# Local attention: the band mask is added by VectorE in PSUM, in place of four TensorE products per tile

## The chip, the cores and the metric

The kernel runs on one core of a Trainium2 chip. The metric is the device time of one execution in microseconds (us); the median of the runs shown counts. A core has TensorE (PE, matrix products, which only write to PSUM), VectorE (DVE), ScalarE (ACT), GpSimd (POOL) and the queue of SyncE (SP) that issues DMA. The engines run on their own instruction streams, each in its order, and meet at semaphores.

## The reference, cut to what matters

The whole is a stack of gated cross-attention layers on x (4, 512, 256) and, as the feed-forward of the last of them, a local transformer of 6 layers. The change concerns its attention: 16 heads of 64 numbers, windows of 64 tokens, each window looking at itself and at the one before it.

```python
def local_attention(q, k, v):
    ...
    bk2, bv2 = (look(bk), look(bv))     # the window before, and the window itself
    ...
    mask = (it < jb) | (it > jb + w) | (jb == -1)
    sim = jnp.einsum('bhwie,bhwje->bhwij', bq, bk2) * QK_SCALE
    sim = jnp.where(mask, -jnp.finfo(sim.dtype).max, sim)
    attn = jax.nn.softmax(sim, -1)
    out = jnp.einsum('bhwij,bhwje->bhwie', attn, bv2)
    return out.reshape(b, h, n, d)
```

A query may see the keys from 64 tokens back up to itself. Around it stand, per layer: `qkv = x @ Wqkv`, l2-norm and rotary embedding of q and k, the output product with `Wo`, and a feed-forward part with layer norm and a gelu gate.

## The kernel before

The kernel has two parts that follow each other. `first_part` does the cross-attention layers and the other feed-forwards; no line of it is touched. `last_part` does the local transformer, from about 2315 us to the end. The change lies in it alone.

**Tiles.** A unit `(d, g, b)` is a layer, a group of four heads and a batch; it has four tiles `tt` of 128 tokens (two windows). That makes 6 x 4 x 4 x 4 = 384 tiles. The order runs through half a layer at a time (two batches, four groups, four tiles each: 32 tiles), so the pattern of work repeats 12 times. I call one such stretch a round.

**Stages of a tile**, each a name in `last_order`, with how many turns after its start it comes: `qkv` (lag 0), `rot` (1), `tr` (3), `sc` and `ex` (4), `pt` (5), `pv` (6), `ot` (7). One turn of the program handles one tile of each stage, so TensorE's stream in a turn is: `wo` (output product, once per unit), `sc`, `tr`, `ot`, `pv`, `pt`, what the feed-forward has in that turn (`fh`, `fw`, the norm), and last `qkv`, which is 12 products (L1300).

**The scores.** `sc` on TensorE first writes the mask and then adds the products to it:

```python
for w in range(2):
    for e in range(2):
        half = slice(64 * e, 64 * e + 64)
        tensor.matmul(psum[64 * w:64 * w + 64, b0 + e, 0:2 * P], ident_b[half, half],
                      bc(band[half, 1 if tt else 0, w, :], 1, 2), start=True, stop=False)
```

These are four products of 64x64 by 256 columns in bf16 (L1318; `w` is the window, `e` the head's parity), one for each quadrant of the array. Eight products of queries by keys follow in fp32 (L1323; 16 instructions in the trace). DVE then takes the maximum per head (L1453, written to a spare corner of PSUM), waits for itself (`step.join()`), and multiplies it into the bias of the exponential (L1457). ACT does four exponentials (`ex`, L1573). The scores have one slot of two banks (`two`), so `sc` of the next tile waits on TensorE for `ex` of this one.

**DVE's stream in a turn**: `wo` (two additions into the residual, L1478), `sc` (L1453, L1457), `rot` (sum of squares, L1447), `ot` (L1471), `pv` (L1464, L1466), the feed-forward's pieces (`fg`: L1510 and the cast L1515), `qkv` (three rotary products, L1439 to L1441), and `lq` (casts of new weights, L1423). **ACT's stream**: `tr` (L1561, L1566), `ot` (L1585), `ex` (L1573), `pt` (L1578), gelu (L1610), `qkv` (copies of v at L1546 to L1551 and the squares L1554, which wait for L1441 and free the bank of q and k). After a gelu the exponential needs its table again: ACT_TABLE_LOAD. **POOL** adds the two rotary parts (L1629), takes the power for the norm (L1633), scales k (L1636) and makes low parts (L1652, L1625).

Six further PSUM banks (`one`) go round in fixed order among `qkv`, `tr`, `pt`, `pv`, `ot`, `wo` and the feed-forward; a stage waits for the engine that last emptied its bank.

Of the kernel before, what the change touches and what calls it, by code (L numbers as in the profile page):

```python
# [7 lines left out]
ALU = mybir.AluOpType  # L8
# [4 lines left out]
BF16 = mybir.dt.bfloat16  # L13
# [4 lines left out]
P = 128  # L18
# [38 lines left out]
def bc(ap, axis, n):  # L57

    dims = [list(d) for d in ap.ap]
    return bass.AP(ap.tensor, ap.offset, dims[:axis] + [[0, n]] + dims[axis:])  # L60
# [1008 lines left out]
def weights_of(d, g, b):  # L1069

    return d, 1 if b >= B // 2 and g < 2 else 0, g
# [54 lines left out]
def last_part(nc, a, at, s):  # L1126

    tensor, vector, scalar, gpsimd, sync = nc.tensor, nc.vector, nc.scalar, nc.gpsimd, nc.sync
    PE, V, A, G, SP = at.PE, at.V, at.A, at.G, at.SP
    vec, sm, psum, tokens = at.vec, at.sm, at.psum, at.tokens  # L1130
    ident, ident_b, ones_mean = at.ident, at.ident_b, at.ones_mean
    order = last_order()
    S_ = {name: s(name) for name in (
        "xs_act xs_pool lq_dve lq_pool rt_dve qk_pe qkv_pe sq_act qkv_act qkv_dve rot_dve rot_pool tr_pe tr_act sc_pe sc_dve ex_act "
        "pt_pe pt_act pv_pe pv_dve ot_pe ot_act ot_dve add_pe add_dve fo_pool fa_pe fa_dve fa_act fa_pool fb_pe fb_dve fb_pool fy_pe fy_dve fc_act fc_dve "
        "fgate_pe fh_pe fh_act fg_dve fi_dve fg_pool fw_pe fx_dve band_in rt_in zeroed fin_dve kept_in written").split()}
    staged_in = [s(f"staged_in{i}") for i in range(2)]
    step = at.step

    with ExitStack() as p2:  # L1140
        def psb(name, shape, dt=F32):
            return p2.enter_context(nc.sbuf_tensor(name, shape, dt))
# [5 lines left out]
        staged = psb("staged", [P, 2, STAGED])  # L1148
        scales = psb("scales", [P, 2, LHD])
        rotary = psb("rotary", [P, 2, 2, QT, 2, LHD])  # L1150
        band = psb("band_bias", [P, 2, 2, P], BF16)
        keys = psb("keys", [P, 1, C, 9 * WIN])
        vals, mixed = psb("vals", [P, 6, 4, LHD + 1]), psb("mixed_vals", [P, 7, 4, LHD + 1])
        queries = psb("queries", [P, 1, C, P])
# [63 lines left out]
        def left(got, key, waits):  # L1218

            before = got[key][1]  # L1220
            if before:
                waits.wait_ge(S_[before[0]], before[1])
# [7 lines left out]
        def stat(name, u):  # L1230
            return stats[:, stat_at[name, u][0], :]
# [5 lines left out]
        def chunk(u):  # L1237

            kind, j = u[0], u[-1]
            if kind == "f":  # L1240
                to = [w[:, j * STAGED:(j + 1) * STAGED] for w in (w12_hi, w12_lo)]
                return a["w12"][u[1]][:, j * STAGED:(j + 1) * STAGED], to
            src = a["quads"][u[1], u[3]]
            if kind == "q":
                to = [w[:, wqkv_at[u[1:4]][0], j * STAGED:(j + 1) * STAGED] for w in (wqkv_hi, wqkv_lo)]
                return src[:, j * STAGED:(j + 1) * STAGED], to
            return src[:, QW:QW + 2 * D], [w[:, wout_at[u[1:4]][0], :] for w in (wout_hi, wout_lo)]
# [12 lines left out]
        def tok(tt):  # L1260
            return slice(tt * P, (tt + 1) * P)
# [11 lines left out]
        def soft(u):  # L1273
            return small_stats[:, soft_at["soft", u][0], :]

        def window_keys(n, e, pair, w):

            even, odd = (w // 2, 4 + w // 2) if w % 2 == 0 else (w // 2, 5 + w // 2)
            part = keys[64 * e:64 * e + 64, n, pair, even * WIN:(even + 1) * WIN]
            dims = [list(d) for d in part.ap]  # L1280
            return bass.AP(part.tensor, part.offset, [dims[0], [(odd - even) * WIN, 2], [1, WIN]])
# [2 lines left out]
            return ap[lo:hi, :, 0:LHD]  # L1284

        def tensor_program():
            PE.wait_ge(S_["band_in"], 16)
            PE.wait_ge(S_["zeroed"], 1)
            for stage, u in order.walk():
                if stage == "qkv":  # L1290
                    d, g, b, tt = u
                    w = weights_of(d, g, b)
# [3 lines left out]
                    for i, (to, lo, hi, sem) in enumerate(((qk, 0, 512, "qk_pe"), (vp[:, 0:256], 512, COLS, "qkv_pe"))):  # L1296
                        left(one, ("qkv", u, i), PE)
                        for c in range(C):
                            for n, (x_, w_) in enumerate(((xs_hi, wh), (xs_hi, wl), (xs_lo, wh))):
                                ins = tensor.matmul(to, x_[:, c, b % 2, tok(tt)], w_[:, c * COLS + lo:c * COLS + hi],  # L1300
                                                    start=c == 0 and n == 0, stop=c == C - 1 and n == 2)
# [8 lines left out]
                elif stage == "sc":  # L1310
                    tt = u[3]
                    PE.wait_ge(S_["tr_act"], at_("tr", u))
                    left(two, u, PE)
                    b0, n, q = two[u][0], key_at["kT", u[:3]][0], queries[:, qry_at["q", u][0], :, :]
                    for w in range(2):
                        for e in range(2):
                            half = slice(64 * e, 64 * e + 64)
                            tensor.matmul(psum[64 * w:64 * w + 64, b0 + e, 0:2 * P], ident_b[half, half],  # L1318
                                          bc(band[half, 1 if tt else 0, w, :], 1, 2), start=True, stop=False)
                    for pair in range(2):  # L1320
                        for w in range(2):
                            for e in range(2):
                                ins = tensor.matmul(psum[64 * w:64 * w + 64, b0 + e, tok(pair)],  # L1323
                                                    q[64 * e:64 * e + 64, pair, 64 * w:64 * w + 64],
                                                    window_keys(n, e, pair, 2 * tt + w), start=False, stop=pair == 1)
                    ins.then_inc(S_["sc_pe"], 1)
                elif stage == "pt":
                    PE.wait_ge(S_["ex_act"], at_("ex", u))
# [22 lines left out]
                elif stage == "wo":  # L1351
                    d, g, b = u
                    PE.wait_ge(S_["ot_dve"], at_("ot", u + (QT - 1,)))
                    w = weights_of(d, g, b)
# [49 lines left out]
        def vector_program():  # L1404
# [4 lines left out]
            for stage, u in order.walk():  # L1409
# [22 lines left out]
                elif stage == "qkv":  # L1432
                    d, g, b, tt = u
# [14 lines left out]
                elif stage == "sc":  # L1448
                    st, y = soft(u), stat("norm", u)[:, 8:12]
                    V.wait_ge(S_["sc_pe"], at_("sc", u))  # L1450
                    left(soft_at, ("soft", u), V)
                    top = psum[:, two[u][0], 2 * P:2 * P + 4].rearrange("p (e j) -> p e j", e=2)
                    step(vector.tensor_reduce(top, scores(u), AX.X, ALU.max))  # L1453
# [14 lines left out]
                elif stage == "ot":  # L1468
                    d, g, b, tt = u
# [183 lines left out]
                                         ALU.subtract).then_inc(S_["fg_pool"], 1)  # L1653

        def sync_program():
            sync.dma_start(band[:, :, :, :], a["band"]).then_inc(S_["band_in"], 16)
            for stage, u in order.walk():
                if stage == "lq":
                    slot = stage_at["lq", u][0]
                    left(stage_at, ("lq", u), SP)  # L1660
                    sync.dma_start(staged[:, slot, :], chunk(u)[0]).then_inc(staged_in[slot], 16)
                elif stage == "rt":
                    if u:
                        SP.wait_ge(S_["rt_dve"], u)
                    if u > 1:
                        SP.wait_ge(S_["qkv_dve"], at_("qkv", (u - 2, 0, B - 1, QT - 1)))
                    sync.dma_start(rotary[:, u % 2], a["rotary"]).then_inc(S_["rt_in"], 16)
                    sync.dma_start(scales[:, :, :], a["qk_scale"][u]).then_inc(S_["rt_in"], 16)
                elif stage == "kb":
                    if u:  # L1670
                        SP.wait_ge(S_["written"], 16 * C * at_("fin", u - 1))
                    for c in range(C):
                        sync.dma_start(back[:, c, :], at.x_kept[c * P:(c + 1) * P, u, :]).then_inc(S_["kept_in"], 16)
                elif stage == "fin":
                    for c in range(C):
                        SP.wait_ge(S_["fin_dve"], C * (at_("fin", u) - 1) + c + 1)
                        sync.dma_start(at.out[c * P:(c + 1) * P, u, :], back[:, c, :]).then_inc(S_["written"], 16)
            SP.wait_ge(S_["written"], 16 * C * B)

        tensor_program()  # L1680
        vector_program()
        scalar_program()
        gpsimd_program()
        sync_program()


# [4 lines left out]
def build(nc, a, out):  # L1691
    ctx = ExitStack()
    with ctx:
# [67 lines left out]
        for w in (PE, V, A, G, SP):  # L1761
            w.wait_ge(at.over, B)
        last_part(nc, a, at, s)


# [6 lines left out]
def lay_out(i):  # L1772
# [5 lines left out]
    a = {}  # L1778
# [42 lines left out]
    bf16 = i["L1_ffn_kernel"].dtype  # L1821
# [3 lines left out]
    n, h = S, LHD // 2  # L1825
    half = np.arange(0, LHD, 2, dtype=np.float32)
# [11 lines left out]
    own, prev = np.where(j_ <= i_, 0.0, MASKED), np.where(j_ >= i_, 0.0, MASKED)  # L1838
    rows = [np.concatenate([own, np.full((WIN, WIN), MASKED)], 1), np.concatenate([own, prev], 1)]
    tiles = np.stack([np.stack([r, np.concatenate([prev, own], 1)]) for r in rows])  # L1840
    a["band"] = np.ascontiguousarray(np.tile(tiles.transpose(2, 0, 1, 3), (2, 1, 1, 1))).astype(bf16)
    qs = np.stack([i["L3_ffn_q_scale"], i["L3_ffn_k_scale"]], 1)
    a["qk_scale"] = np.ascontiguousarray(np.broadcast_to(qs[:, None], (DEPTH, P, 2, LHD)))
    wqkv = i["L3_ffn_Wqkv"].reshape(DEPTH, D, 3, 4, 4 * LHD).transpose(0, 3, 1, 2, 4).reshape(DEPTH, 4, D, 12 * LHD)
# [4 lines left out]
    for k in range(2):  # L1849
        w = np.zeros((DEPTH, D, HT * P), np.float32)  # L1850
# [19 lines left out]
```

## Time and profile before

| | |
|---|---|
| median of three runs | 5177.25 us (5173.41 to 5180.86) |
| span of the profiled execution | 5182.7 us |
| busy over the span: PE, DVE, ACT, POOL | 93%, 66%, 60%, 46% |
| tiles of local attention | 384, from about 2333 us to the end |

The profiled execution is 5.4 us longer than the median of the runs. In the profile "busy" of PE counts from the start of each product to a modelled end, so that it contains short gaps. An idle time has behind it, after `<-`, what ended it; "issue" is time in which nothing shown was waited for.

### The profile page before, as it was taken

How to read it: one execution, taken by the hardware profiler on the slowest of the kernel's cores; microseconds unless marked ns; L12 is line 12 of the kernel's file. 1: busy time of each engine (PE TensorE's matmuls, PEld its weight loads, DVE VectorE, ACT ScalarE, POOL GpSimd, SP SyncE). 2: the span in 40 equal slices, each digit the busy share in tenths (PEclk: the TensorE clock that was granted, in tenths of full speed). 3: DMA queues.
4: the chain of work that ended last, by engine and by line, in shares of the span. 5: the costliest groups of instructions: out<-in, count | busy, mean ns of one | idle time of the engine just before them, and what ended most of it. 6: DMA issues, size and time to landing. Idle time of an engine off the chain costs nothing.

```text
span 5182.7 us, 92467 instructions
## 1 busy us (share of the span) xinstructions
PE 4823.6 (93%) x35414; PEld 3013.7 (58%) x35480; DVE 3429.4 (66%) x6514; ACT 3112.6 (60%) x6618; POOL 2409.7 (46%) x2314
## 2 busy tenths in 40 slices
PE   6898999989899898969999999999999999999998
PEld 2232333334334343227877777777777777777776
DVE  4766566676675857757766666666666666666664
ACT  3565555434344444547777677776777677777763
POOL 3211101111011111129777677676767677776762
PEclk8999999999999899989999999999999999999998
DMA  5233222322312222311000000000000000000000
GB/s 121 52 56 59 54 44 55 65 50 48 61 37 50 46 57 43 56 30 46 8 18 26 16 24 20 22 22 20 22 18 24 18 28 16 24 19 19 24 22 21
DMA packets 125161, 188.97 MB, mean 36 GB/s; under 512 B 18896, under 2 KB 67664, under 8 KB 124496
## 3 DMA queue, kind: packets, MB, share of 16 engines
q1 hardware_dynamic: 124720, 183.06, 15.9%
q8 instruction: 281, 4.60, 0.4%
q14 instruction: 160, 1.31, 0.1%
HBM read 150.09 MB, written 32.51 MB: 35 GB/s over the span
## 4 chain that ended last, share of the span: by engine, by line
PE 64%; DVE 14%; ACT 8%; POOL 7%; issue 6%; DMA 1%; SPq 0%; DVEq 0%; POOLq 0%; ACTq 0%
PE psum L1253 16%; PE psum L1300 10%; PE psum L467 4%; PE psum L432 4%; PE psum L453 4%; DVE maxes L655 3%; PE psum L1308 3%; PE psum L1341 3%; PE psum L1332 2%; PE psum L414 2%; PE psum L1323 2%; POOL stats L1633 2%; PE psum L476 2%; ACT probs L836 2%; PE psum L422 1%
## 5 line engine op out<-in xcount | busy, mean ns | idle before, releaser
L836 ACT ACTIVATE probs<-psum 128x1024 f32<-128x1024 f32 x768 | 772.2, 1019 | 609.9 <-PE psum L453 337.7
L655 DVE TENSOR_REDUCE maxes<-psum 128x1 f32<-128x1024 f32 x512 | 616.5, 1212 | 246.6 <-PE psum L432 242.5
L1633 POOL TENSOR_TENSOR stats<-stats,minus_half 128x8 f32<-128x8 f32 x384 | 651.8, 1697 | 32.0
L1439 DVE TENSOR_TENSOR lwork<-psum,rotary 128x512 f32<-128x512 f32 x384 | 264.2, 688 | 513.1 <-PE psum L1300 446.9
L1573 ACT ACTIVATE lprobs<-psum,small_stats,stats 128x128 f32<-128x128 f32 x1536 | 581.1, 474 | 12.3 <-DVE small_stats L1457 11.5
L1629 POOL TENSOR_TENSOR lwork<-lwork 128x512 f32<-128x512 f32 x384 | 493.9, 1286 | 202.9 <-DVE lwork L1441 202.7
L1300 PE MATMUL psum<-wqkv_hi,xs_hi 128*128 128x512 f32 (+1 forms) x1536 | 554.6, 361 | 33.6 <-POOL xs_lo L1620 17.1
L453 PE MATMUL psum<-stack 98*128 98x512 bf16 x1536 | 513.1, 390 | 72.1 <-DVE maxes L655 32.0
L432 PE MATMUL psum<-stack 96*128 96x512 bf16 x1536 | 473.2, 391 | 64.2 <-ACT probs L836 53.1
L1300 PE MATMUL psum<-wqkv_hi,xs_lo 128*128 128x512 f32 (+1 forms) x1536 | 519.6, 338 | 0.0
L1300 PE MATMUL psum<-wqkv_lo,xs_hi 128*128 128x512 f32 (+1 forms) x1536 | 519.3, 338 | 0.0
L957 POOL TENSOR_TENSOR attn<-attn,sums 128x512 f32<-128x512 f32 x48 | 60.9, 1268 | 948.4 <-DVE sums L688 948.4
L467 PE MATMUL psum<-probs,values 128*32 128x512 f32 x3072 | 428.2, 631 | 0.7 <-ACT probs L836 0.6
L1546 ACT ACTIVATE vals<-psum 128x256 f32<-128x256 f32 x384 | 152.9, 398 | 452.6 <-PE psum L1300 451.2
L652 DVE CUSTOM_DVE_ANT_0 psum<-psum,mask_by_query 128x1024 f32<-128x1024 f32 x256 | 314.1, 1228 | 151.9 <-PE psum L432 150.2
L453 PEld LDWEIGHTS psum<-stack 98*128 98x128 bf16 x1536 | 135.9, 100 | 427.9 <-issue 183.2
L1300 PEld LDWEIGHTS psum<-wqkv_hi,xs_hi 128*128 128x128 f32 x1536 | 291.1, 190 | 96.9 <-issue 33.5
L432 PEld LDWEIGHTS psum<-stack 96*128 96x128 bf16 x1536 | 131.6, 99 | 357.9 <-ACT probs L836 131.3
L1300 PEld LDWEIGHTS psum<-wqkv_lo,xs_hi 128*128 128x128 f32 x1536 | 291.5, 190 | 42.1 <-issue 5.3
L1300 PEld LDWEIGHTS psum<-wqkv_hi,xs_lo 128*128 128x128 f32 x1536 | 290.3, 189 | 33.4
L1554 ACT ACTIVATE lwork<-psum 128x512 f32<-128x512 f32 x384 | 225.6, 587 | 135.7 <-DVE lwork L1441 133.5
L1447 DVE TENSOR_REDUCE stats<-lwork 128x8 f32<-128x512 f32 x384 | 263.4, 686 | 26.8 <-ACT lwork L1554 23.0
(225 smaller groups left out, 11526.7 us busy)
## 6 DMA issues: line engine op xcount, KB each, us to landing
stack<-k_parts SPq DMA_DIRECT2D x288, 128.0 KB
staged<-in_quads SPq DMA_DIRECT2D x144, 256.0 KB, 3.0
k_parts<-parts SPq DMA_DIRECT2D x48, 384.0 KB, 2.9
stack<-q_parts SPq DMA_DIRECT2D x288, 64.0 KB
staged<-in_w SPq DMA_DIRECT2D x54, 256.0 KB, 2.7
ctx<-in_ctxT SPq DMA_DIRECT2D x24, 512.0 KB, 4.7
q_parts<-parts SPq DMA_DIRECT2D x24, 384.0 KB, 2.3
arena<-in_ctxT SPq DMA_DIRECT2D x8, 512.0 KB, 4.8
```

The lines of the kernel that those rows point to most:

```text
L432: ins = tensor.matmul(ps[:, i, :], q[0:STACK, h, qt * P:(qt + 1) * P], k[0:STACK, h, i * S:(i + 1) * S], start=True, stop=True)
L453: ins = tensor.matmul(ps[:, i, :], ky[0:STACK + 2, h, kt * P:(kt + 1) * P], q[0:STACK + 2, h, :], start=True, stop=L != 1)
L467: ins = tensor.matmul(bank(acc)[32 * h:32 * h + 32, :], values[:, kt, 4 * g + h, :], pr, start=kt == 0, stop=kt == KT - 1)
L652: ins = vector.tensor_tensor_reduce(out=scores, in0=scores, in1=masks_q[:, qt * S2:(qt + 1) * S2], scale=1.0, scalar=-3e38, op0=ALU.add, o ...
L655: ins = vector.tensor_reduce(to, pair(("M", u)), AX.XY, ALU.max)
L836: scalar.activation(probs[:, i % 6, :, :], pair(("E", u)), ACT.Exp).then_inc(S_["E_act"], 1)
L1253: ins = tensor.matmul(ps, l, r, start=first and n == 0, stop=last and n == 2)
L1300: ins = tensor.matmul(to, x_[:, c, b % 2, tok(tt)], w_[:, c * COLS + lo:c * COLS + hi], start=c == 0 and n == 0, stop=c == C - 1 and n == 2)
L1439: vector.tensor_tensor(v4(t1), v4(qk), bc(rotary[:, d % 2, 0, tt], 2, 4), ALU.mult)
L1573: ins = scalar.activation(pr[:, h, :], scores(u)[:, h % 2, h // 2, :], ACT.Exp, bias=st[:, 4 + h:5 + h], scale=y[:, h:h + 1])
L1629: gpsimd.tensor_tensor(t1, t1, t2, ALU.add)
L1633: pool_step(gpsimd.tensor_tensor(st[:, 8:16], st[:, 0:8], minus_half[:, :], ALU.pow))
```

## The change

The four products that write the mask are gone; the eight products of queries by keys now each start afresh (`start=True, stop=True`). `band` is laid out by rows of the tile, 128 partitions by 128 columns for each of its two forms, and holds the same values (0 and -1e30, bf16). On DVE `sc` gets one more instruction, which adds `band`, spread over the four heads, to the 512 columns of scores in place in PSUM, and a join, so that the maximum waits for it. The wait for the DMA of `band` moves from TensorE to DVE. No other stage is moved.

```diff
-            PE.wait_ge(S_["band_in"], 16)
             PE.wait_ge(S_["zeroed"], 1)
...
-                    for w in range(2):
-                        for e in range(2):
-                            half = slice(64 * e, 64 * e + 64)
-                            tensor.matmul(psum[64 * w:64 * w + 64, b0 + e, 0:2 * P], ident_b[half, half],
-                                          bc(band[half, 1 if tt else 0, w, :], 1, 2), start=True, stop=False)
                     for pair in range(2):
                         for w in range(2):
                             for e in range(2):
                                 ins = tensor.matmul(psum[64 * w:64 * w + 64, b0 + e, tok(pair)],
                                                     q[64 * e:64 * e + 64, pair, 64 * w:64 * w + 64],
-                                                    window_keys(n, e, pair, 2 * tt + w), start=False, stop=pair == 1)
+                                                    window_keys(n, e, pair, 2 * tt + w), start=True, stop=True)
                     ins.then_inc(S_["sc_pe"], 1)
...
                     st, y = soft(u), stat("norm", u)[:, 8:12]
                     V.wait_ge(S_["sc_pe"], at_("sc", u))
+                    V.wait_ge(S_["band_in"], 16)
+                    of_tile = bc(bc(band[:, 1 if u[3] else 0, :], 1, 2), 1, 2)
+                    step(vector.tensor_tensor(scores(u), scores(u), of_tile, ALU.add))
+                    step.join()
                     left(soft_at, ("soft", u), V)
                     top = psum[:, two[u][0], 2 * P:2 * P + 4].rearrange("p (e j) -> p e j", e=2)
                     step(vector.tensor_reduce(top, scores(u), AX.X, ALU.max))
...
-            sync.dma_start(band[:, :, :, :], a["band"]).then_inc(S_["band_in"], 16)
+            sync.dma_start(band[:, :, :], a["band"]).then_inc(S_["band_in"], 16)
```

DVE's rows around the scores of one tile, in the kernel before:

```order
L1478 TENSOR_TENSOR x_resid<-psum,x_resid 128x512 [waits add_pe]
L1478 TENSOR_TENSOR x_resid<-psum,x_resid 128x512
L1453 TENSOR_REDUCE psum<-psum 128x4 [waits pv_dve,sc_pe]
L1457 SCALAR_TENSOR_TENSOR small_stats<-psum,stats 128x2x2 [waits vector_step]
L1447 TENSOR_REDUCE stats<-lwork 128x8 [waits ex_act,sq_act]
```

The same place in the changed kernel, where lines have other numbers:

```order
L1476 TENSOR_TENSOR x_resid<-psum,x_resid 128x512 [waits add_pe]
L1476 TENSOR_TENSOR x_resid<-psum,x_resid 128x512
L1447 TENSOR_TENSOR psum<-psum,band_bias 128x2x256 [waits sc_pe]
L1451 TENSOR_REDUCE psum<-psum 128x4 [waits pv_dve,vector_step]
L1455 SCALAR_TENSOR_TENSOR small_stats<-psum,stats 128x2x2 [waits vector_step]
L1441 TENSOR_REDUCE stats<-lwork 128x8 [waits ex_act,sq_act]
```

The wait for the scores has gone from the maximum to the addition, and the maximum waits for DVE's own step. On ACT nothing is added; its rows at the exponential, in a turn that follows a gelu, are in the kernel before:

```order
L1585 ACTIVATE att_hi<-psum 128x2x128 [waits ot_pe]
L1573 ACT_TABLE_LOAD
L1573 ACTIVATE lprobs<-psum,small_stats,stats 128x128 [waits sc_dve]
L1573 ACTIVATE lprobs<-psum,small_stats,stats 128x128 x3
L1578 ACTIVATE turned<-psum 128x512 [waits pt_pe]
```

The load of the table stands ahead of the wait for DVE.

## Rows read from the trace of the kernel before

**Rows 1.** The page: span, and busy time of each engine.

```profile
span 5182.7 us, 92467 instructions
PE 4823.6 (93%) x35414; PEld 3013.7 (58%) x35480; DVE 3429.4 (66%) x6514; ACT 3112.6 (60%) x6618; POOL 2409.7 (46%) x2314
```

**Rows 2.** Busy time by stretch, local attention: us, busy us (instructions), PEclk, DMA share, GB/s.

```profile
2700.00:5100.00 2400.00, 2350.43 (x22207) 1883.79 (x22206) 1613.65 (x3690) 1704.72 (x4497) 1711.56 (x1676) 1.00 0.07 21
```

**Rows 3.** Waits in 2700 to 5100 us: who waited for whom, us in total, times, longest.

```profile
DVE lwork L1439 <- PE psum L1300: 393.9, 145, 6.1
PE psum L1318 <- ACT lprobs L1573: 18.6, 51, 0.4
ACT lprobs L1573 <- DVE small_stats L1457: 8.9, 17, 2.0
```

**Rows 4.** PE in order of time, one tile's scores: start us, us, engine, line, operation.

```profile
3535.51 0.30 PE L1318 MATMUL psum<-band_bias,ident_b 64*64 64x256 bf16 x4
3535.63 0.62 PE L1323 MATMUL psum<-keys,queries 64*64 64x128 f32 x16
```

**Rows 5.** Groups by line in 2700 to 5100 us: busy us, mean ns of one, idle before.

```profile
L1318 PE MATMUL psum<-band_bias,ident_b 64*64 64x256 bf16 x1300 | 98.5, 293 | 18.6 <-ACT lprobs L1573 18.6
L1478 DVE TENSOR_TENSOR x_resid<-psum,x_resid 128x512 f32<-128x512 f32 x164 | 105.5, 686 | 103.3 <-PE psum L1253 103.3
```

**Rows 6.** In order of time, DVE, ACT and PE, a tile far from feed-forward work.

```profile
3210.34 0.16 DVE L1457 SCALAR_TENSOR_TENSOR small_stats<-psum,stats 128x4 f32<-128x4 f32 x1
3212.48 0.69 DVE L1439 TENSOR_TENSOR lwork<-psum,rotary 128x512 f32<-128x512 f32 x1 [0.50 <-PE psum L1300]
...
3210.53 1.51 ACT L1573 ACTIVATE lprobs<-psum,small_stats,stats 128x128 f32<-128x128 f32 x4
...
3213.08 0.30 PE L1318 MATMUL psum<-band_bias,ident_b 64*64 64x256 bf16 x4
```

**Rows 7.** DVE in order of time, two tiles after a gelu.

```profile
3055.75 0.69 DVE L1453 TENSOR_REDUCE psum<-psum 128x4 f32<-128x512 f32 x1
3056.47 0.16 DVE L1457 SCALAR_TENSOR_TENSOR small_stats<-psum,stats 128x4 f32<-128x4 f32 x1
...
3060.27 0.68 DVE L1439 TENSOR_TENSOR lwork<-psum,rotary 128x512 f32<-128x512 f32 x1
3060.87 0.41 DVE L1440 TENSOR_TENSOR lwork<-psum,rotary 128x256 f32<-128x256 f32 x1
...
3061.53 0.69 DVE L1453 TENSOR_REDUCE psum<-psum 128x4 f32<-128x512 f32 x1
3062.26 0.16 DVE L1457 SCALAR_TENSOR_TENSOR small_stats<-psum,stats 128x4 f32<-128x4 f32 x1
```

**Rows 8.** ACT and PE in order of time, the same two tiles.

```profile
3056.82 1.28 ACT L1573 ACT_TABLE_LOAD   x1
3058.11 1.50 ACT L1573 ACTIVATE lprobs<-psum,small_stats,stats 128x128 f32<-128x128 f32 x4
...
3062.98 1.54 ACT L1573 ACTIVATE lprobs<-psum,small_stats,stats 128x128 f32<-128x128 f32 x4
...
3059.67 0.30 PE L1318 MATMUL psum<-band_bias,ident_b 64*64 64x256 bf16 x4 [0.38 <-ACT lprobs L1573]
...
3064.66 0.30 PE L1318 MATMUL psum<-band_bias,ident_b 64*64 64x256 bf16 x4
```

**Rows 9.** Two other places of the round: DVE at 3033; ACT and PE at 3162.

```profile
3033.01 0.69 DVE L1447 TENSOR_REDUCE stats<-lwork 128x8 f32<-128x512 f32 x1 [0.27 <-issue]
...
3162.72 1.54 ACT L1573 ACTIVATE lprobs<-psum,small_stats,stats 128x128 f32<-128x128 f32 x4
...
3164.49 0.30 PE L1318 MATMUL psum<-band_bias,ident_b 64*64 64x256 bf16 x4
```

**Rows 10.** In order of time, a wait of PE for a bank, and what leads to it.

```profile
3132.75 0.42 DVE L1471 TENSOR_TENSOR att_lo<-psum,att_hi 128x256 fp32r<-128x256 f32 x1 [0.18 <-ACT att_hi L1585]
...
3138.39 0.60 ACT L1554 ACTIVATE lwork<-psum 128x512 f32<-128x512 f32 x1 [1.32 <-DVE lwork L1441]
...
3139.04 0.50 PE L1300 MATMUL psum<-wqkv_hi,xs_hi 128*128 128x512 f32 x1 [0.71 <-ACT lwork L1554]
```

More of the change, by code:

```diff
@@ L1150, in last_part @@
         rotary = psb("rotary", [P, 2, 2, QT, 2, LHD])
-        band = psb("band_bias", [P, 2, 2, P], BF16)
+        band = psb("band_bias", [P, 2, P], BF16)
         keys = psb("keys", [P, 1, C, 9 * WIN])
@@ L1840, in lay_out @@
     tiles = np.stack([np.stack([r, np.concatenate([prev, own], 1)]) for r in rows])
-    a["band"] = np.ascontiguousarray(np.tile(tiles.transpose(2, 0, 1, 3), (2, 1, 1, 1))).astype(bf16)
+    a["band"] = np.ascontiguousarray(tiles.transpose(1, 2, 0, 3).reshape(P, 2, P)).astype(bf16)
     qs = np.stack([i["L3_ffn_q_scale"], i["L3_ffn_k_scale"]], 1)
```

## The prediction

> **What bounds the kernel now.** I read the page first, then the local attention's stretch alone, then the waits in it, then single tiles in order of time. The page has PE at 93% and DVE at 66% of a span of 5182.7 us [rows 1]. In the stretch that the change touches PE is busy for 2350 of 2400 us at a granted clock of 1.00 (the 2.4 GHz level), DVE for 1614, ACT for 1705 and POOL for 1712 [rows 2]. So TensorE sets the pace there, and whatever leaves its stream is worth its full time wherever PE is not waiting for anyone. The waits show the other half: DVE waits for PE's qkv products in 145 turns of some 325, for 394 us [rows 3]. In the other turns it is behind PE, with work queued. And PE already waits for an exponential 51 times, 18.6 us in all, which is about five times in each round of 32 tiles [rows 3]. The reader is to look, place by place, at how far the chain scores, maximum, exponential, next scores is from PE's own pace. The change shortens PE's part and lengthens DVE's part of that chain.
>
> **What is removed: four products.** Their rows say 293 ns each [rows 5], but the four run at once in their quadrants and the next products do not wait for their ends: the first product of queries by keys starts 0.12 us after the first of the four, 3535.63 against 3535.51 [rows 4]. That is what a tile gives back, 0.12 us; 384 tiles would make 46 us if PE waited nowhere. As bounds I take 0.10, the same with a slightly longer first load of fp32 weights now in the open, and 0.30, the length of the group's whole row [rows 4]. I take 0.12, since the distance of two starts leaves out the modelled ends.
>
> **What is added: one DVE instruction and its join.** Before has no in-place addition in PSUM. The nearest row is the residual's addition, a 128x512 fp32 operation with one PSUM operand, 686 ns [rows 5]. With a join behind it the next instruction starts 0.73 us after (the maximum at 3061.53, its successor at 3062.26), where without one two rotary products start 0.60 apart (3060.27 and 3060.87) [rows 7]. The maximum must wait for the sum, so I take 0.73 per tile. The bounds are 0.60, as if the join were free, and 1.0, an estimate: one operation's 0.69 plus half again for reading and writing the same bank, which no row shows. Over 384 tiles that is 280 us more of DVE, on 3429 [rows 1]; it makes DVE 74% over the stretch (1614 + 325 x 0.73 = 1851 of 2400), so that DVE doesn't become the bound as a whole. The question is where it is late already.
>
> The Trainium skill (VectorE: DVE Perf Modes, "The DRAIN you can't avoid") says that the next DVE instruction starts only when the pipe is empty, and that a semaphore between two costs nothing extra. The two distances above, 0.60 and 0.73, disagree with it in this case. By that rule with the unjoined distance, the addition would cost 0.60, and the sum below would come out 12 us lower, at 5172; I keep the row with the join.
>
> **Where the addition is covered.** Behind the addition wait the maximum, L1457, everything else of DVE's turn, ACT's exponential, and through it PE's next scores; through DVE's rotary products (L1439 to L1441) ACT's squares, and through them a bank for PE; and POOL's sums. In a tile far from feed-forward work [rows 6] the exponential ends at 3212.04 and PE comes for the slot at 3213.08: 1.04 us of cover for 0.73. DVE then waits 0.50 for PE before L1439, so that about 0.2 us, and the 0.12 by which PE is earlier, are carried on; the next such wait or the next long turn takes them. In turns with feed-forward products or the output product DVE waits for microseconds (394 us in 145 waits, rows 3), and all is absorbed. If this cover were gone, each tile would cost 0.6. In the turn right after a gelu, PE waits for the exponential (0.38 at 3059.67), but there the load of the table, 1.28 us, stands ahead of the wait for DVE [rows 8]: L1457 ends at 3056.63, the exponential starts at 3058.11, and 1.48 us of cover are enough.
>
> **Where it is not covered.** The second tile after a gelu. DVE runs from the maximum at 3055.75 to the one at 3061.53 without a wait [rows 7], since it has two pieces of the gate between. Two additions fall into this stretch, 1.46 us. Their cover is what lies between L1457's end (3062.42) and the exponential (3062.98), 0.56, less 0.04 for the handover, and between the exponential's end (3064.52) and PE's scores (3064.66), 0.14, less 0.05 [rows 8]. That leaves 1.46 - 0.52 - 0.09 = 0.85 us late for PE, and PE is the pace here, so that it is not made up. A round has four such places. At 3001 to 3012 the rows repeat these two covers: 0.85. At 3162 the second cover is 0.23 instead of 0.14 [rows 9]: 0.76. At 3033 there are 0.27 us of idle DVE in between [rows 9]: 0.58. The sum is 3.0 us per round, 36 us over 12 rounds.
>
> Besides, PE waits 0.71 for a bank that ACT's squares free, and these wait 1.32 for DVE's L1441 [rows 10]. One addition lies ahead of it and 0.18 of a DVE wait covers it (and some 0.05 more): 0.5 late, 6 us over 12 rounds.
>
> **The sum.** The 0.12 is realised in the 24 tiles of a round that are not part of one of the four chains: 24 x 0.12 x 12 = 35 us less. So 36 + 6 - 35 = 7 us more. Of the profiled 5182.7 that makes 5189.7, and since that execution stood 5.4 us above the median of the runs, 5184.
>
> The moved wait for the mask's DMA costs nothing: it was issued at the head of the last part, and the first scores come four turns later. POOL gets the sums of squares up to 0.73 later and has one more turn until PE needs its result. What first_part does is unchanged.
>
> **Rivals.**
> (a) *The mask's products occupy PE longer than the two starts say.* If a tile gives back 0.24 (between 0.12 and the row's 0.30 [rows 4]), the gain is 24 x 0.24 x 12 = 69 and the price the same 42: 27 us less, 5150. For it: 0.12 is about the streaming of 256 columns alone, and a change of operand type at the switch may cost something. Against it: the distance is the same wherever I looked at a tile.
> (b) *The covers hold.* The four places lose nothing because the delay moves phases of POOL and DVE or because DVE takes the slack elsewhere: 384 x 0.12 = 46 less, 5131. For it: PE's long turns reset DVE. Against it: in rows 7 DVE has no gap at all. A milder form of it is the free join, 12 us less than the forecast.
> (c) *The addition costs more than 0.73, and DVE is behind in every short turn.* Decisive price: in the short turn of rows 6 DVE has 0.50 us of its own plus what PE leaves; from 0.9 us on each short turn hands on its delay instead of absorbing it. At 1.0 us the four places cost 4 x (2.0 - 0.61) less 0.36 = 5.2 per round and the bank place 0.8, 72 us in 12 rounds, against 35: 37 us more, 5214. For it: reading and writing the same PSUM bank has no row. Against it: the residual's addition shows no surcharge for its PSUM operand.
> (d) *More places are uncovered than four.* DVE was behind PE in over half of the turns (180 of 325, rows 3). If two more tiles of a round lose 0.6 each, it is 14 us more than the forecast, 5198.
>
> **How the numbers follow.** About 0.2% (10 us) is what a measurement of this kernel can tell from no change. The forecast, with its neighbours from the free join to one place more (5172 to 5192), has a chance of 0.45; (d) 0.20; (c) 0.13; (a) 0.14; (b) 0.08. The forecast's own spread reaches past 5187 with a third of its chance. Faster by over 0.2% (below 5167): (a) and (b), 0.22. Slower by over 0.2% (above 5187.6): (c), (d) and some 0.07 of the forecast's, 0.40. The rest is 0.38. The range from 5145 to 5216 holds (a), the forecast, (d) and the price in (c), and leaves out (b) and the far end of (c).
>
> **What would show it.** Scores of a tile starting about 0.12 earlier behind the last qkv product confirms the gain; the distance from the addition's start to the maximum's should be 0.73. PE's wait for the exponential should grow from 18.6 us to some 50 in the same stretch, at four new places per round, and the wait of L1300 for the squares by 0.5 at one. DVE's wait for L1300 should shrink by over 150 us. I am wrong if PE waits for the exponential in quiet tiles as well, or if the addition takes over 0.8.

## The result, and the profile after

| | before | changed |
|---|---|---|
| median of the runs | 5178.91 us | 5224.27 us |
| span of the profiled execution | 5182.7 us | 5224.8 us |

The changed kernel is slower, by under 1% but clear of noise. The ratio is 1.0085, 95% interval 1.0071 to 1.0099: 44 us more, 37 to 51. That lies outside the range from 5145 to 5216.

The page after, and the stretch of local attention alone (us, busy us of PE, PEld, DVE, ACT, POOL, granted clock, DMA share, GB/s), which answer to [rows 1] and [rows 2]:

```profile
span 5224.8 us, 89780 instructions
PE 4812.3 (92%) x33878; PEld 2985.4 (57%) x33944; DVE 3652.1 (70%) x6898; ACT 3134.0 (60%) x6618; POOL 2409.9 (46%) x2314
...
2700.00:5100.00 2400.00, 2310.08 (x20588) 1835.47 (x20587) 1774.31 (x3959) 1703.89 (x4445) 1699.53 (x1665) 1.00 0.07 21
```

PE is busy 40 us less in 2400, at the same granted clock of 1.00 (the 2.4 GHz level), so the clock has no part in it. The first scores start within 4 us of where they did; the whole loss comes after. The waits of the same stretch, which answer to [rows 3]:

```profile
DVE lwork L1433 <- PE psum L1299: 332.9, 101, 5.3
ACT lprobs L1571 <- DVE small_stats L1455: 76.1, 119, 2.7
PE psum L1299 <- ACT lwork L1552: 28.9, 51, 0.9
PE psum L1317 <- ACT lprobs L1571: 20.0, 80, 0.4
PE psum L1253 <- ACT lwork L1552: 14.2, 29, 0.9
```

PE's wait for the exponential has hardly grown, from 18.6 to 20.0 us, though it comes 80 times instead of 51. What has grown is PE's wait for the squares (lwork, L1552), which free a bank. In the kernel before these were:

```profile
PE psum L1300 <- ACT lwork L1554: 15.6, 27, 0.7
PE psum L1341 <- ACT lwork L1554: 5.2, 20, 0.3
PE psum L1253 <- ACT lwork L1554: 1.1, 5, 0.2
```

To see where the time went I compared the distance from one tile's first score product to the next one's in both traces, tile by tile, and took the mean over ten rounds (the second to the eleventh, 320 distances). Tiles of a round are counted from 0.

| place in the round | 4 | 5 | 6 | 9 | 12 | 20 | 22 | 25 | 28 | 18 places, each | all 32 |
|---|---|---|---|---|---|---|---|---|---|---|---|
| change, us per round | +0.62 | +0.72 | +0.25 | +0.88 | +0.98 | +0.57 | -0.34 | +0.38 | +0.82 | -0.07 or -0.08 | +3.9 |

Seven places (4, 5, 9, 12, 20, 25, 28) lose 5.0 us per round, and place 6 another 0.25. The five places that the table leaves out (1, 3, 14, 21, 26) add 0.3 together. A tile in which PE waits for nobody is 0.07 shorter, not 0.12. Twelve rounds of 3.9 make 47 us; the first round loses nothing, and from the first scores to the end the changed kernel takes 46 us more.

Three of these means hide two kinds of round. A round is half a layer, and the two halves differ. In second halves place 25 loses 1.16 and place 22 loses 0.22; in first halves they gain 0.40 and 0.91. Place 9 loses 0.60 in second halves and 1.16 in first ones. The reason at places 22 and 25 is told below, under "Two places where a cast is in play".

**The gain.** PE in order of time, a tile away from feed-forward work, first before, then after (start us, us):

```profile
3213.08 0.30 PE L1318 MATMUL psum<-band_bias,ident_b 64*64 64x256 bf16 x4
3213.21 0.61 PE L1323 MATMUL psum<-keys,queries 64*64 64x128 f32 x16
3213.75 0.33 PE L1308 MATMUL psum<-ident,lwork 128*128 128x128 f32 x1
```

```profile
3209.61 0.67 PE L1317 MATMUL psum<-keys,queries 64*64 64x128 f32 x16
3210.20 0.33 PE L1307 MATMUL psum<-ident,lwork 128*128 128x128 f32 x1
```

From the first product to the transposes behind it takes 0.67 before and 0.59 after. The products by the keys themselves took 0.54 before and take 0.59 now: the 0.13 of the mask's products covered 0.05 or 0.06 of them. The first loads of fp32 weights used to run beside the mask's products and now stand in the open; in the starts of single products the first group of four holds the array for 0.16 us, each later one for 0.11.

**The addition** costs what was forecast. DVE after, two tiles behind a gelu:

```profile
3061.55 0.69 DVE L1447 TENSOR_TENSOR psum<-psum,band_bias 128x512 f32<-128x512 f32 x1
3062.27 0.70 DVE L1451 TENSOR_REDUCE psum<-psum 128x4 f32<-128x512 f32 x1
```

0.72 us from start to start, and no surcharge for reading and writing one bank.

**The loss, at place 12** (the second tile after a gelu, [rows 7, 8] before). ACT and PE before, then after:

```profile
3061.65 0.60 ACT L1554 ACTIVATE lwork<-psum 128x512 f32<-128x512 f32 x1 [1.03 <-DVE lwork L1441]
...
3061.76 0.66 PE L1332 MATMUL psum<-ident,lprobs 128*128 128x128 f32 x4
3062.39 0.47 PE L1300 MATMUL psum<-wqkv_hi,xs_hi 128*128 128x512 f32 x1
```

```profile
3068.19 0.60 ACT L1552 ACTIVATE lwork<-psum 128x512 f32<-128x512 f32 x1 [1.84 <-DVE lwork L1435]
...
3068.93 0.47 PE L1299 MATMUL psum<-wqkv_hi,xs_hi 128*128 128x512 f32 x1 [0.86 <-ACT lwork L1552]
```

After, the squares end at 3068.79 and PE starts its qkv products 0.14 later. Before, they end at 3062.25, and PE starts 0.14 later as well, at 3062.39. So PE was waiting for this bank already, and no row said so: the transposes in front of it (L1332) have a modelled end at 3062.42, later than the next start, so that no idle time shows. Their starts show it. In the quiet tile of [rows 6] qkv follows the transposes at 0.42 (3210.39 and 3210.81), here at 0.63. The cover was nil. (A cover is the time by which something may come late before anyone waits for it.) At place 28 the same holds of the products of the feed-forward; before, then after:

```profile
3183.84 0.60 ACT L1554 ACTIVATE lwork<-psum 128x512 f32<-128x512 f32 x1 [1.02 <-DVE lwork L1441]
...
3183.97 0.66 PE L1332 MATMUL psum<-ident,lprobs 128*128 128x128 f32 x4
3184.49 0.50 PE L1253 MATMUL psum<-hid_hi,w_hi 128*128 128x512 f32 x1
```

```profile
3192.81 0.60 ACT L1552 ACTIVATE lwork<-psum 128x512 f32<-128x512 f32 x1 [1.82 <-DVE lwork L1435]
...
3193.46 0.50 PE L1253 MATMUL psum<-hid_hi,w_hi 128*128 128x512 f32 x1 [0.75 <-ACT lwork L1552]
```

0.05 from the squares' end to PE in both (3184.44 and 3184.49; 3193.41 and 3193.46), and the forecast had this turn among the long ones that absorb everything.

The same reading at all seven places: in the changed kernel PE starts 0.05 us (5, 9, 25, 28) or 0.14 us (4, 12, 20) after the end of the squares, in round after round, so PE is held by their bank at each of them. In the kernel before the distance is already 0.14 at place 12 and 0.05 at place 28. At place 20 it is 0.39, which leaves 0.25 of cover. At place 4 it is 0.5 in half of the rounds and 0.14 in the others, and place 9 has 0.18 of cover in half of them and none in the rest. What makes the handover 0.05 at one place and 0.14 at another the runs do not show.

**Two places where a cast is in play.** Before, a DVE cast of the gate's result (L1515) took 1.55 us instead of 0.43 in 17 of its executions: at place 22 in every round but the first, just ahead of place 25 in first halves of a layer, and once more in the last round. Each time a GpSimd row of L1652 starts within 4 ns of it; in 11 others that row starts some 40 ns later, and the cast takes 0.43. The cast makes DVE's rotary products late and so the squares' bank. Before, place 25:

```profile
2923.41 1.55 DVE L1515 CAST hid_hi<-lwork 128x512 fp32r<-128x512 f32 x1
2923.41 1.27 POOL L1652 TENSOR_TENSOR hid_lo<-lwork,hid_hi 128x512 fp32r<-128x512 f32 x1
...
2926.91 0.50 PE L1300 MATMUL psum<-wqkv_hi,xs_hi 128*128 128x512 f32 x1 [0.69 <-ACT lwork L1554]
```

In the changed kernel the two no longer start together, and all 17 are gone. In second halves others come up: ahead of place 25 the cast takes 0.70, and at place 22 a cast of weights takes 1.47, with a GpSimd row that started 0.04 to 0.09 ahead of it, and PE waits for another result of DVE. After, place 22:

```profile
3144.23 1.48 DVE L1417 CAST wqkv_hi<-staged 128x512 fp32r<-128x512 f32 x1
...
3148.24 0.50 PE L1253 MATMUL psum<-att_hi,wout_hi 128*128 128x512 f32 x1 [0.88 <-DVE att_lo L1469]
```

So the 44 us contain a gain that comes from shifted starts and not from the mask.

### The profile page after: what moved, and what is told of

It is laid out like the page before. It is cut to its first block, busy times and chain, and to the rows that moved or that the text cites. A ratio compares the mean times of both kernels' runs of the same rounds, so it can differ in the third digit from the quotient of the medians.

```text
span 5224.8 us, 89780 instructions
## 1 busy us (share of the span) xinstructions
PE 4812.3 (92%) x33878; PEld 2985.4 (57%) x33944; DVE 3652.1 (70%) x6898; ACT 3134.0 (60%) x6618; POOL 2409.9 (46%) x2314
## 4 chain that ended last, share of the span: by engine, by line
PE 57%; DVE 22%; issue 7%; ACT 7%; POOL 6%; DMA 1%; SPq 0%; DVEq 0%; POOLq 0%; ACTq 0%
PE psum L1253 16%; PE psum L1299 8%; PE psum L467 4%; PE psum L432 4%; PE psum L453 4%; DVE maxes L655 3%; PE psum L414 2%; DVE psum L1451 2%; POOL stats L1631 2%; PE psum L476 2%; PE psum L1335 2%; DVE psum L1447 2%; PE psum L1326 2%; DVE lwork L1433 2%; ACT probs L836 2%
## 5 line engine op out<-in xcount | busy, mean ns | idle before, releaser
L1552 ACT ACTIVATE lwork<-psum 128x512 f32<-128x512 f32 x384 | 225.7, 588 | 183.1 <-DVE lwork L1435 181.4
L1317 PE MATMUL psum<-keys,queries 64*64 64x128 f32 x6144 | 256.4, 282 | 29.5 <-ACT lprobs L1571 23.3
```

## The experiments

The theory from the traces: PE pays where it waits without cover for a bank that ACT's squares free, since the addition delays DVE's rotary products; the removal brings 0.07 per tile. The rivals: the price is paid through the exponential, as forecast; or the addition harms all tiles (a busier DVE, PSUM contended).

### Removal alone, addition alone

The changed kernel without its addition (the mask is left out), and the kernel before with the addition too.

```diff
                     V.wait_ge(S_["sc_pe"], at_("sc", u))
-                    V.wait_ge(S_["band_in"], 16)
-                    of_tile = bc(bc(band[:, 1 if u[3] else 0, :], 1, 2), 1, 2)
-                    step(vector.tensor_tensor(scores(u), scores(u), of_tile, ALU.add))
-                    step.join()
                     left(soft_at, ("soft", u), V)
```

> The changed kernel without its addition and join: the band mask is left out altogether, so this is the removal of the four products alone. In the trace of the changed kernel a covered tile's turn is 0.07 us shorter than before, not 0.12. If that is all a tile gives back, the time is 384 x 0.07 = 27 us below before, near 5152. If the forecast's 0.12 held, 46 us below, near 5133. If leaving out the products itself did harm, it would be at or above before.

Measured: 0.9963 (0.9950 to 0.9976), 19 us less, 12 to 26. In its trace 19 of the 32 places of a round are 0.07 shorter. The others give 0.05 at most or lose (place 6 0.17, places 12 and 28 0.08), which makes 1.05 us per round, 13 us in twelve. Its profiled execution is 19 us shorter than the one before, and 6 of these stand ahead of the first scores, in code that is the same. The 27 us lie at the upper end, and the forecast's 46 are out.

> The kernel before with the addition and its join on VectorE as in the change, the four products kept (the mask is added twice, which leaves the result as it is). If gain and price add up (gain 27 of removal alone, 45 net), the price alone is about 72: near 5250. If the shorter TensorE turn itself makes VectorE late and so causes part of the price, the addition alone costs less, 45 to 60: 5225 to 5240. The forecast's own price of 42 would give 5221.

Measured: 1.0097 (1.0082 to 1.0112), 50 us more. The same places pay (4: 0.54, 5: 0.71, 9: 0.81, 12: 0.90, 20: 0.49, 25: 0.35, 28: 0.74 per round), places 3 and 6 lose 0.15 and 0.24, place 22 gains 0.26, and the rest keep their length to 0.05 us, most of them to 0.01. A price in all tiles is thereby excluded. By the runs the two parts add to 31 against 44 of the change, with some 7 of uncertainty on each of the three. The traces leave less of a gap: -1.05 and +4.70 us per round add to 3.65 against 3.90, 3 us in twelve rounds. So the two parts nearly add; five of the seven places pay 0.07 or 0.08 more when PE comes earlier.

### Ahead of the exponential or behind it

First with an operation of two inputs in SBUF (`back` is a buffer that only the last layer uses):

```diff
+                    if u[0] < DEPTH - 1:
+                        V.wait_ge(S_["band_in"], 16)
+                        spare = back[:, 0, :].rearrange("p (h n) -> p h n", h=4)
+                        step(vector.tensor_tensor(spare, spare, bc(band[:, 1, 0, :], 1, 4), ALU.max))
+                        step.join()
```

> The kernel before with one addition-like operation of the same size (128x512 fp32, in SBUF, joined) ahead of the maximum, in the 320 tiles of the first five layers. Both theories: 5/6 of what the addition alone costs, some 60 us, 5239, if reading and writing PSUM in place has no price of its own. If it has, this comes out clearly lower than 5/6 of the addition alone.

> The same operation, but behind the last instruction of the scores on VectorE, so that the exponential of the tile doesn't wait for it, while the rotary products, ScalarE's squares and the bank they free do. If the price is paid through VectorE's whole turn and the bank (the theory from the trace of the changed kernel), it costs nearly what it costs ahead of the maximum, 45 to 60 us. If it is paid on the way scores, maximum, exponential, next scores, as forecast, it costs under half of that, below 30 us.

Measured: 1.0164 (1.0147 to 1.0181), 85 us more ahead; 1.0169 (1.0154 to 1.0184), 88 us behind. That is far above what was expected (some 60 ahead; 45 to 60, or below 30, behind), and twice the 42 that are 5/6 of the addition's 50. So the probe itself was not clean. Its rows, ahead and behind (duration in ns: minimum, median, maximum):

```profile
L1455 DVE TENSOR_TENSOR x_back<-x_back,band_bias x320: 671/685/1826, 2332.7 to 4703.6; 128x512 f32<-128x512 f32 x160
```

```profile
L1463 DVE TENSOR_TENSOR x_back<-x_back,band_bias x320: 681/1173/3473, 2331.1 to 4709.0; 128x512 f32<-128x512 f32 x160
```

An operation of 0.69 us took up to 3.5. The pair was repeated with a maximum over 512 columns of SBUF, which has one input:

```diff
+                    if u[0] < DEPTH - 1:
+                        step(vector.tensor_reduce(back[:, 1, 0:8], back[:, 0, :].rearrange("p (h n) -> p h n", h=8), AX.X, ALU.max))
+                        step.join()
```

> The kernel before with one more maximum over 512 columns of SBUF (one input only, joined, the same 0.69 us) ahead of the maximum of the scores, in the 320 tiles of the first five layers. The operation with two inputs in SBUF cost 84 us at this place, and its own rows grew to 0.86 us on average where GpSimd was at work. If that contention was the surplus, this one costs 5/6 of the addition in PSUM alone, 42 us: 5220. If working in place in PSUM saves or costs something, it lies off that.

> The same operation behind the last instruction of the scores. The exponential of the tile no longer waits for it, the rotary products and ScalarE's squares do. If TensorE pays for the bank that the squares free, this costs 30 to 42 us, nearly what it costs ahead. If it pays for the exponential, below 15 us.

Measured: ahead 1.0093 (1.0077 to 1.0108), 48 us more; behind 1.0083 (1.0069 to 1.0096), 43 us more. Here every instance took 668 to 687 ns. Ahead of the maximum it costs 5/6 of the addition (42 us) within the noise, so that working in place in PSUM shows no price of its own. Behind it costs nearly the same, where the path through the exponential would have given below 15. The waits of both in 2700 to 5100 us, ahead first, then behind:

```profile
ACT lprobs L1577 <- DVE small_stats L1461: 58.4, 101, 2.3
PE psum L1300 <- ACT lwork L1558: 22.7, 40, 1.1
PE psum L1318 <- ACT lprobs L1577: 21.4, 74, 0.4
```

```profile
PE psum L1300 <- ACT lwork L1558: 22.8, 40, 1.2
PE psum L1318 <- ACT lprobs L1577: 17.7, 50, 0.4
ACT lprobs L1577 <- DVE small_stats L1458: 10.2, 20, 2.0
```

Behind, the exponential is as free as in the kernel before (10.2 us of waits, against 8.9 in [rows 3]), and PE waits for the squares' bank as long as ahead. The path through the exponential is thus worth about the 5 us between the two, with some 10 of uncertainty; at place 12, where it should matter most, the operation costs 0.88 ahead and 0.71 behind in the first five layers. The bank is the price.

### A narrow addition

The kernel before with an addition over 64 columns.

```diff
+                    narrow = scores(u)[:, :, 0, 0:32]
+                    step(vector.tensor_tensor(narrow, narrow, bc(band_rows[:, 1 if u[3] else 0, 0:32], 1, 2), ALU.add))
+                    step.join()
```

> The kernel before with a joined addition over 64 columns in place of 512 ahead of the maximum (the mask twice in those columns, which changes nothing): some 0.2 us of VectorE per tile. By the covers of the forecast (0.6 us behind the two tiles after a gelu) it costs nothing: within 3 us of before. If at seven places of a round TensorE waits for a bank without any cover, it costs 7 x 0.2 x 12 = 17 us.

Measured: 1.0017 (1.0008 to 1.0026), 9 us more, between the two expectations. It took 0.26 us with its join. Place by place it settles what the total doesn't: places 12 and 28 lose 0.27 and 0.28 per round, the full price, so these have no cover at all. Place 20 loses 0.03, as its cover of 0.25 says. Places 4, 5 and 9 lose 0.10 to 0.12 on the mean: 4 and 5 lose 0.2 in second halves of a layer and nothing in first ones, 9 loses 0.05 and 0.18. Place 6 loses 0.19. Place 25 gains 0.42, for in first halves its cast takes 0.43 here instead of 1.55 and brings 1.02. The bank at place 12, ACT and PE:

```profile
3053.33 0.60 ACT L1559 ACTIVATE lwork<-psum 128x512 f32<-128x512 f32 x1 [1.30 <-DVE lwork L1442]
...
3054.07 0.47 PE L1301 MATMUL psum<-wqkv_hi,xs_hi 128*128 128x512 f32 x1 [0.25 <-ACT lwork L1559]
```

The same 0.14 from the squares' end to PE as in both kernels.

### Half the addition, and twice

The half adds the mask to two of the four heads and leaves the others unmasked; for twice, the addition and its join stand there a second time, which leaves the result as it is. The edit of the half:

```diff
-                    of_tile = bc(bc(band[:, 1 if u[3] else 0, :], 1, 2), 1, 2)
-                    step(vector.tensor_tensor(scores(u), scores(u), of_tile, ALU.add))
+                    half_of = psum[:, two[u][0]:two[u][0] + 2, 0:P]
+                    step(vector.tensor_tensor(half_of, half_of, bc(band[:, 1 if u[3] else 0, :], 1, 2), ALU.add))
```

> The changed kernel with the mask added to two of the four heads only (256 columns, some 0.47 us with its join); the other two heads go unmasked. Without an addition the time was 19 us below before, with the whole one 45 above. If the price is VectorE's time at places without cover, it is linear in between: 19 below plus 0.47 x 88 us per us, 22 above, near 5201. If a part of the price is the additional join and instruction itself, it lies higher, above 5210.

> The changed kernel with the joined addition twice (the mask twice, which leaves the result as it is). If only the same places pay, 0.73 us more at seven places of a round is 61 us more: 5285. If covers of up to 1 us at other places are used up by now, the slope is steeper: 5300 to 5340. Below 5260 would speak against a price paid in VectorE's time.

Measured: half 1.0021 (1.0011 to 1.0030), 11 us more than before; twice 1.0370 (1.0356 to 1.0385), 192 us more. Against DVE's additional time per tile:

| added on DVE per tile, us | 0 | 0.46 | 0.73 | 1.46 |
|---|---|---|---|---|
| against before, us | -19 | +11 | +44 | +192 |
| slope to the next, us per us | 65 | 122 | 203 | |
| in the traces, us per round | -1.05 | +1.10 | +3.90 | +16.25 |

Against what was expected of the half, the price is not linear: it lies below the 22 of the straight line, and it bends upward as covers run out. At 1.46 the covered places pay too (place 0: 0.39, place 18: 1.06, place 31: 0.56 per round), and the steeper of the two expectations was still too flat, by far. The full slope, if every tile paid, would be 384.

### The addition only where it is covered

Products in some tiles, additions in the others.

```diff
+PRODUCT_AT = (3, 4, 5, 8, 9, 11, 12, 19, 20, 21, 24, 25, 27, 28)
...
+        def by_product(u):
+
+            return (order.nth["sc", u] - 1) % 32 in PRODUCT_AT
...
-                    for w in range(2):
+                    for w in range(2 if by_product(u) else 0):
...
-                                                    window_keys(n, e, pair, 2 * tt + w), start=False, stop=pair == 1)
+                                                    window_keys(n, e, pair, 2 * tt + w), start=not by_product(u), stop=pair == 1 or not by_product(u))
...
+                    if not by_product(u):
+                        V.wait_ge(S_["band_in"], 32)
+                        of_tile = bc(bc(band_rows[:, 1 if u[3] else 0, :], 1, 2), 1, 2)
+                        step(vector.tensor_tensor(scores(u), scores(u), of_tile, ALU.add))
+                        step.join()
```

> The addition on VectorE in 18 of the 32 tiles of a round, the four products kept in the 14 (counted from 0: 3, 4, 5, 8, 9, 11, 12, 19, 20, 21, 24, 25, 27, 28) behind which TensorE came late in the changed kernel. If the price is paid only where a bank or the scores' slot has no cover, each of the 18 tiles brings 0.07 us and nothing is lost: 12 x 18 x 0.07 = 15 us below before, 5162 to 5172. If the price is spread over all tiles (VectorE busier, or PSUM contended), it stays at 18/32 of the loss of the whole change, some 20 us above before.

Measured: 1.0004 (0.9995 to 1.0013), no difference from before, where 15 us less were expected. The 44 us are gone, with additions in 18 tiles of 32, so the price is not spread over all tiles. The gain did not come whole: 13 places are 0.07 or 0.08 shorter, while places 1, 3 and 6 lose 0.22, 0.17 and 0.09. A second set of tiles has products at 31, 0, 1 and 2 also:

> As the mixed version, but with the products kept also at the four tiles 31, 0, 1 and 2 of a round, ahead of the places where the mixed version still came late by 0.2 us. Additions are left in 14 tiles: 12 x 14 x 0.07 = 12 us below before if nothing is lost, 5168. If what a tile brings is eaten by TensorE's own waits, as in half of the places so far, it is within 5 us of before.

Measured: 0.9987 (0.9978 to 0.9996), 7 us less, 2 to 11. All of the losing places are at zero or 0.01 to 0.04, and the ten that gain give 0.07 each (0.7 us per round). It is faster than both kernels; against the kernel before the amount is at the edge of what can be measured.

## Why the prediction was wrong

- **The gain per tile.** Measured 0.07, forecast 0.12, with 0.10 as the lower bound. The step that failed is the reading of two starts as the group's price. The term was mis-sized: the load that then stands in the open takes 0.05 back, and the bound allowed 0.02 for it. With fewer tiles realising it (19 of 32 instead of 24) the removal alone brought 19 us by the runs and 13 by its trace, not 35.
- **The addition's price, 0.73.** Right. 0.72 in the trace, no surcharge in PSUM. (The 74% of DVE beside it is a slip: 1851 of 2400 are 77%.)
- **The four uncovered places** were named right (5, 9, 12, 25 of a round), and their sum was 3.0 us per round against 0.72 + 0.88 + 0.98 + 0.38 = 2.96. The path was wrong. I subtracted 0.05 and took the rest of 0.14 between the exponential and the next scores as cover; the distance is 0.14 there in round after round of both traces, so all of it is handover. PE comes late through the bank first, and only the remainder (some 0.2 at place 12) through the exponential. The two paths share DVE's delay, so the sizes had to be alike. That the sum came out to 0.1 is luck: place 9 costs 0.3 more than forecast and place 25 0.4 less, and the latter is the mean of +1.16 and -0.40, with a cast in play.
- **The places taken as covered.** This is the step that made the result: "In turns with feed-forward products or the output product DVE waits for microseconds (394 us in 145 waits, rows 3), and all is absorbed". DVE's own wait absorbs the delay for what comes behind it on DVE. But the squares come before that, and in the middle of the long turn PE comes for their bank: at place 28 it stood there already, at place 20 it had 0.25 of cover, and at place 4 0.4 in half of the rounds and none in the others. The addition's 0.73 is more than any of these. Places 4, 20 and 28 lose 2.0 us per round, 24 us in all, which I had at nothing. The profile shows no idle time of PE at place 28, because the modelled end of the transposes lies beyond the next start; at places 4 and 20 only the distance from the squares' end to PE could have given a warning. Rival (d), two more uncovered tiles of 0.6 each, named this without its place; it had 0.20 and stopped at 5198.
- **The bank place, 22.** Forecast 0.5 more per round, measured 0.34 less. The wait of 0.71 in [rows 10] stood behind a cast of 1.55 us that had started together with a GpSimd row. The forecast took it as fixed. In the changed kernel that cast takes 0.43: first halves of a layer gain 0.91, and second halves lose 0.22, because there another cast grows to 1.47.
- **The sum with the measured terms,** per round: -1.3 for 18 shorter tiles, +2.96 at the four places, +2.01 at the three taken as covered, +0.58 at places 1, 3, 6 and 26, and -0.34 at place 22. That is +3.9, where the forecast had +0.7.
- **Signs named in advance:** PE's wait for the exponential was to grow to some 50 us (it is 20.0), DVE's wait for L1300 was to shrink by over 150 (393.9 to 332.9, 61). Both say that I had the wrong wait. The free join, by which the Trainium skill (VectorE: DVE Perf Modes, "The DRAIN you can't avoid") would have had 5172, is not borne out: 0.72 stands between the joined addition and the maximum, and 0.60 between rotary products without a join [rows 7]. The same section adds that a next operation which is not held starts earlier, and the 0.60 agrees with that; the forecast's reading of the page left it out.

## What to carry to other kernels

Before a delay on a helper engine is called covered, look at the starts of the bounding engine behind every bank and buffer that the helper frees, and compare the same pair of instructions in a quiet turn: a modelled end can hide the wait, and an equal distance from the helper's end in several places is a handover, not a cover. Work moved off the bounding engine brings the distance between starts with and without it, less the load that it was covering. Waits that depend on which of two engines starts first can appear or vanish with any edit, and a mean over unlike rounds hides them. And where a price is paid only at some turns of a fixed pattern, the move can be made for the other turns alone.

## What the runs showed of the hardware

- An fp32 operation on VectorE with two inputs in SBUF slows down beside GpSimd and slows GpSimd down. 128x512 took 681 to 684 ns where no GpSimd row overlapped it, and a median of 1173 ns, up to 3473, behind the scores, where GpSimd was mostly at work; GpSimd's own 128x512 sum took 1.75 us at the 90th percentile, against 1.30 before. The one-input maximum took 668 to 687 in the same places, and the addition with one input in PSUM 677 to 700. The Trainium skill (GPSIMD Engine Reference, "1. Specifications") says that GpSimd's SBUF interfaces are shared with VectorE and contended by VectorE instructions with two SBUF inputs or in a 2-port mode. The trace agrees for two inputs, and the cost to the kernel was 85 us instead of 48.
- A cast with one input in SBUF can be held up as well: 1.55 us instead of 0.43 for 128x512 in all 17 cases in which a GpSimd row of L1652 started within 4 ns of it, and 0.43 in the 11 in which that row started some 40 ns later. No run varied the two starts on purpose.
- In-place addition in PSUM is as fast as an addition that only reads it: 691 ns at the median, beside 686 on the mean for the residual's [rows 5].
